# Keys parts among the gates, keys copies behind the cross exponentials, and the first cross maxima ahead of a product, in a decoder block on one core

## What is computed

```python
x = x + self_attention(layernorm(x))       # 32 heads of 64, 8 key heads, rope, window of 32 back, causal
x = x + cross_attention(layernorm(x), ctx) # 16 heads of 16, k and v expanded from a latent of 64, causal
x = x + ffn(layernorm(x))                  # silu(x @ w_gate) * (x @ w_up), best 2 of every 4 kept, @ w_down
```

## Time and profile before

| | |
|---|---|
| median of 3 runs | 402.59 us (402.5 to 402.78) |
| the profiled execution | 402.36 us, of which the span from first to last instruction is 400.6 us |
| PE matmul busy | 384.2 us (96% of the span) |
| DVE busy | 288.0 us (72%) |
| ACT busy | 214.2 us (53%) |
| POOL busy | 170.7 us (43%) |
| mean granted clock of PE | 0.999 |

### The profile page before, as it was taken

How to read it: one execution, slowest core, us unless ns; L and a number is a source line. 1 busy time by engine, 2 the same in 40 slices (tenths; PEclk the granted TensorE clock), 3 DMA queues, 4 the chain that set the end, 5 groups by cost and what they waited for, 6 DMA issues and landing times.

```text
span 400.6 us, 8280 instructions
## 1 busy us (share of the span) xinstructions
PE 384.2 (96%) x3080; PEld 315.7 (79%) x3080; DVE 288.0 (72%) x627; ACT 214.2 (53%) x549; POOL 170.7 (43%) x169
## 2 busy tenths in 40 slices
PE   8999999899999999999999999999999899999997
PEld 7768778667799777877789877877779779866795
DVE  4879922878769974779959977478877974686374
ACT  1465844588434842387444663177643756188330
POOL 5553779478411450267620440067831520057000
PEclk9999999999999999999999999999999999999999
DMA  7985531304001301351000400352000400200000
GB/s 209 343 359 187 174 97 67 114 34 97 3 15 52 107 2 49 111 151 55 2 15 0 132 29 26 106 152 54 2 2 31 127 2 3 79 0 2 28 0 28
DMA packets 21894, 30.48 MB, mean 76 GB/s; under 512 B 2528, under 2 KB 15712, under 8 KB 21600
## 3 DMA queue, kind: packets, MB, share of 16 engines
q1 hardware_dynamic: 21856, 29.96, 23.8%
HBM read 22.88 MB, written 7.08 MB: 75 GB/s over the span
## 4 chain that ended last, share of the span: by engine, by line
PE 54%; DVE 23%; issue 8%; ACT 7%; POOL 7%; DMA 1%; POOLq 0%; DVEq 0%; ACTq 0%
PE ps L694 13%; PE ps L775 7%; PE ps L634 5%; DVE rope L1014 4%; ACT prob L1463 4%; POOL prob L1319 4%; DVE mx L1043 3%; PE ps L655 3%; DVE total L1057 3%; PE ps L569 3%; PE ps L560 2%; PE ps L791 2%; PE ps L552 2%; PE ps L733 2%; PE ps L680 2%
## 5 line engine op out<-in xcount | busy, mean ns | idle before, releaser
L1319 POOL TENSOR_TENSOR prob<-prob,inv 128x512 f32<-128x512 f32 x80 | 82.8, 1041 | 82.1 <-DVE inv L1063 82.1
L1463 ACT ACTIVATE prob<-ps,mx 128x128 f32<-128x128 f32 (+1 forms) x128 | 52.6, 429 | 16.3 <-DVE mx L1041 13.1
L694 PE MATMUL ps<-wo_sb,qs 128*128 128x256 f32 x256 | 59.8, 380 | 0.0
L1312 POOL TENSOR_TENSOR qs<-rope 128x512 f32<-128x512 f32 x31 | 39.6, 1277 | 38.8 <-DVE rope L1014 37.0
L634 PE MATMUL ps<-ident_sb,prob 128*128 128x128 f32 x320 | 49.7, 278 | 3.9 <-POOL prob L1319 3.3
L694 PEld LDWEIGHTS ps<-wo_sb,qs 128*128 128x128 f32 x256 | 46.8, 190 | 6.8 <-issue 1.6
L1478 ACT ACTIVATE pT<-ps 128x512 f32<-128x512 f32 x76 | 45.5, 599 | 9.9 <-PE ps L634 9.4
L1014 DVE TENSOR_TENSOR rope<-ps,trig_sb 64x512 f32<-64x512 f32 x70 | 48.2, 688 | 0.9
L634 PEld LDWEIGHTS ps<-ident_sb,prob 128*128 128x128 f32 x320 | 36.6, 141 | 12.7 <-POOL prob L1319 8.7
L1305 POOL TENSOR_TENSOR rstd<-vareps,power 128x1 f32<-128x1 f32 x24 | 13.1, 552 | 64.6 <-DVE vareps L993 64.2
L1041 DVE TENSOR_REDUCE mx<-ps 128x2 f32<-128x512 f32 (+1 forms) x48 | 32.7, 688 | 8.3 <-PE ps L614 7.5
(11 more groups left out here) (169 smaller groups left out, 803.8 us busy)
## 6 DMA issues: line engine op xcount, KB each, us to landing
k<-kx SPq DMA_DIRECT2D x32, 128.0 KB, 3.0
q<-qx SPq DMA_DIRECT2D x28, 128.0 KB, 2.6
work<-in_wgu SPq DMA_DIRECT2D x4, 512.0 KB, 8.1
wo_sb<-in_wo SPq DMA_DIRECT2D x1, 2048.0 KB, 13.8
vx<-pT SPq DMA_DIRECT2D x7, 256.0 KB, 2.5
wq_raw<-in_wqk SPq DMA_DIRECT2D x3, 512.0 KB, 7.9
vb<-vx SPq DMA_DIRECT2D x6, 256.0 KB, 4.5
vb<-vx SPq DMA_DIRECT2D x6, 224.0 KB, 4.7
```

The lines of the kernel that those rows point to most:

```text
L694: mm = pe.matmul(half_banks(use, b)[:, 0, :], window_o[t][:, pair, r, :], wo_sb[:, pair, r, :], start=(pair == 0 and r == 0), stop=(pair = ...
L1312: pool.tensor_tensor(to, cos, sin, ALU.add).then_inc(s_sums, 1)
L1319: pool.tensor_tensor(p, p, inv[:, i % ND, 0:g].unsqueeze(2).broadcast_to([P, g, 512 // g]), ALU.mult).then_inc(s_norm, 1)
L1463: ins = act.activation(prob[:, i % ND, h * k:(h + 1) * k], ps[:, BANK_S + i % 2, h * k:(h + 1) * k], ACT.Exp, bias=mx[:, i % ND, h:h + 1], ...
```

## The change

Three moves, all for rows 0 to 2. No arithmetic is added or removed.

1. The high part of the next row's latent keys is copied by ACT before the gates' silu instead of behind the next row's first window exponentials, and DVE makes the low part behind the product of q7, ahead of the gate products, instead of inside the first window units.
2. ACT copies the keys groups (`keys`) behind the exponentials of cross units 0 and 1. Before, the first was copied ahead of unit 0's and the second ahead of unit 1's.
3. DVE takes the maxima of cross unit 0 ahead of the rope product of k1 instead of behind it.

In DVE's program (`first_units`, then `batch`):

```diff
-                    if i == (1 if b else HEAD - 1):
+                    if prior is None and i == HEAD - 1:
                         keys_rest(prior)
...
                 queries_rest(b, 1)
-                if more:
-                    next_group("k1", b, 2)
                 for i in range(XU + LAG_V):
                     if i < XU:
                         unit_max(b, NQB + i)
+                    if i == 0 and more:
+                        next_group("k1", b, 2)
...
                 if more:
                     next_group("q7", b, 10)
+                    keys_rest(b)
```

In ACT's `batch`:

```diff
-                    if more:
-                        if t:
-                            keys(0, RG * (b + 1) + 1)
-                        elif b:
-                            v_copy("v1", b, 1)
+                    if more and b and t == 0:
+                        v_copy("v1", b, 1)
                 for i in range(XU + LAG_T):
...
                     if i < XU:
                         unit_exp(b, NQB + i)
-                    if i == 0 and more:
-                        keys(1, RG * (b + 1) + 2)
+                    if i < GROUPS and more:
+                        keys(i, RG * (b + 1) + 1 + i)
...
                 act.activation(x3_hi[:], half_banks("ln3", b), ACT.Copy).then_inc(s_x3hi, 1)
+                if more:
+                    latent_keys(b)
...
                 if more:
-                    unit_exp(b + 1, 0)
-                    latent_keys(b)
-                    for i in range(1, HEAD):
+                    for i in range(HEAD):
                         unit_exp(b + 1, i)
```

## The result

The changed kernel takes 399.12 us (median of 6 runs, 399.01 to 399.55) against 402.71 us for the kernel before on the same chip (402.5 to 402.84, 6 runs): 3.6 us less, ratio 0.9903 with a 95% interval of 0.9874 to 0.9932. The forecast was 398.8 in a range of 397.7 to 400.2. Run once more beside the last experiments, it took 399.25 (398.95 to 399.3), ratio 0.9908 (0.9876 to 0.9940).

The account below looks back on a forecast made before the run. PE, busy 96% of the span, was taken as the bound, its waits as what reordering can win. Cross stage 2.7 plus window units 1.1 is 3.8 us, taking 402.59 to 398.8 us, range 397.7 to 400.2.

Parts of the forecast that it names:

- Moves 2 and 3: Cross stage: PE's waits at the scores of units 2 and 3 go; rows 0, 1, 2 win 0.7, 1.0, 1.0, sum 2.7.
- The rival that the gain is given back later: Cross stage: DVE's q products and POOL's additions bind instead of PE; each stage wins 0.56, giving 399.8; 17%.
- forecast margin of 0.07: Cross unit 5's maxima, rows 1 and 2: DVE ready at 178.85, PE at 178.92, so PE still releases them.
- Row 0: Row 0's cross stage: unit 4's scores come up against unit 2's exponentials, so 0.7 is won, not 0.99 and more.
- Move 1: Window units: 0.57 off DVE's chain, capped by PE's scores, wins 0.33, 0.33 and 0.4 in rows 1 to 3, sum 1.1.
- The gates: Work added among the gates is hidden and costs 0; the silu is at most 0.34 late.
- the 0.2 over: Ahead of the first gate product: DVE's idle 0.78 hides the added 0.57, with 0.2 over.
- The slower rival: Head of the gates: silu late, first gate's bank not free, PE stops; 404.8 us at a lateness of 4 us; 4%.
- its cover of some 2: In the gates, lateness is covered by 2.16 on DVE and about 2 on PE.
- Its price: Past some 2 us of lateness in the gates, the cost is 1 for 1 in three rows.

Follow-up runs that it names:

- the cap lifted in rows 1 and 2: Changed kernel with PE making window unit 3's scores ahead of the last down product in rows 1 and 2: 398.78 us.
- four more operations: Changed kernel with four more low-part operations on DVE among the gates in rows 0 to 2: 400.96 us.
- six: Changed kernel with six more low-part operations on DVE among the gates in rows 0 to 2: 407.45 us.
- the next two changes: On the changed kernel: row 0's unit 2 maxima ahead of q0's product, 398.56 us; window unit 3's scores ahead of the last down product, 398.78 us.
- the one with both changes: Changed kernel with row 0's unit 2 maxima before q0's product and window unit 3's scores before the last down product (rows 1, 2): 398.55 us.

## Why the prediction was right

**Moves 2 and 3.** The chain in rows 1 and 2 was the forecast one: maxima when the scores are there, exponentials, keys copy, exponentials. Its gain was 0.98 and 0.99 for 1.0. That it takes both orders was implied by the working (the copy and the product each stand in front of the other's consumer), and the runs with one move show it: 2.9 slower with move 2, and no gain with move 3. The rival that the gain is given back later, since DVE wins only 0.56, didn't come about: at unit 5 DVE and PE met, with no idle time left. Of the forecast margin of 0.07 nothing remained, and it was still enough: PE waits for nothing behind it. How much later DVE could have been before PE pays is not shown.

**Row 0** is the term that was mis-sized: 0.7 forecast, 0.51 measured. The place was right, unit 4's scores wait for unit 2's exponentials (1.02). The forecast took the exponentials as over 1.38 + 0.05 behind their start. In the trace they start at 80.63 and PE is released at 82.19, 1.56. The last one is followed by its own accumulator read, which ends at 81.92 + 0.21 = 82.13, and 1.38 is only the distance at which the next operation can start. That is 0.13 of the missing 0.2. The rest is q0's product, whose wait for the keys copy ends a little later, so that unit 2's maxima win 0.50 and not 0.57.

**Move 1.** 0.30, 0.31 and 0.40 for 0.33, 0.33 and 0.4. That a chain shortened by 0.57 wins 0.3 because PE's scores come next was argued. The runs bear it out at the place: with the cap lifted in rows 1 and 2, DVE's idle time at unit 3 is gone and PE's wait at unit 5's transposes 0.26 and 0.29 shorter. What that is worth behind it is less sure, 0.2 in the trace and 0.5 in the median.

**The gates** took the added work for nothing, and would have taken 2.2 more. The first gate product isn't late at all; the 0.2 over was 0.07. The silu starts at 204.12. The 205.43 of before, less the 1.60 by which PE was ahead at that place, is 203.83: 0.29 late, forecast at most 0.34. On the table load the trace again has 1.28 and a silu 1.29 behind its start. The 2.66 of the Trainium skill, ScalarE: Activation LUTs, section What ACT_TABLE_LOAD costs, isn't seen here either.

**The slower rival** named the right place, PE's bank, and its cover of some 2 was right: four more operations of 0.72 are 2.9, and PE waits 0.7, so 2.2 are covered; six are 4.3, and PE waits 2.2. DVE's idle time of 2.16 is the same cover seen from its side. Its price was not right. It counted three rows alike. With four more operations only rows 0 and 1 pay; with six, row 2's lateness is paid too, in the window units of row 3 and with 1.3 instead of 2.2. And it knew nothing of the clock, with whose fall behind the longer stop row 0 lost 1.6 more than row 1. It didn't matter to the sum.

**Startup.** The terms add up to 3.8 and the stages to 3.5; 0.2 of the missing 0.3 is row 0. The trace's span has 3.3 of these 3.5, because of the -0.19 of the first stretch, which no term covers; in the median's 3.6 that stretch varies from one execution to the next. That the median came out closer to the forecast than the stages did is luck.

## What to carry to other kernels

When a consumer waits behind another instruction on two engines, move both: of these orders one alone made the kernel 2.9 slower and the other alone won nothing, because the copy and the product stand in each other's way. Size a gain by what comes next at that place, not by the time of what is taken away: 0.57 off a chain gave 0.3, and the next two changes of the same kind follow from the idle times that the profile after shows. An idle stretch in front of an instruction is cover for work only as far as the buffers behind it allow: count when PE wants the bank back.

## What the runs showed of the hardware

A stop of PE of 2.20 us between gate products was followed by some three microseconds at the lower clock level (granted clock 0.50 from 117.50 to 120.50) in one place, and by no fall at all in another place of the same execution with the same stop. In the traces, stops of 0.7 and 1.14 brought no fall. That doesn't make them safe: the mean granted clock was 0.996, as with one such stretch, in one of eleven executions with the stops of 0.7, and also in three executions of the kernel before (405.85, 406.06 and 406.28 us, over 3 above its median). None of these four was traced, so what precedes the fall there is open.

Until PE's first scores, executions of the same instructions differ by up to 0.6 us, over half of what move 1 is worth. The stages behind mostly agree to a few hundredths. Between the end of a cross stage and the next window units, in rows 0 and 1, 0.1 comes and goes; and an execution can wait for a transfer, as the one with both changes did for the cross queries, 0.80 in row 0 and 0.76 in row 1.
